# Gated linear attention with routed experts: a chunk's output products on quarters of TensorE's array, copied out by ScalarE, and the work behind them re-ordered

## The reference, cut to what matters

```
q = relu(x @ Wq)   16 heads of 64        k = relu(x @ Wk), v = x @ Wv   4 key heads of 64
g = log_sigmoid(x @ Wg1 @ Wg2 + b) / 16
S_t = exp(g_t) * S_(t-1) + k_t (outer) v_t ;  o_t = q_t @ S_t / 8
o = g_norm_weight * o * rsqrt(mean(o^2 over the head) + eps)
x = x + layernorm(o @ Wo)
x = x + layernorm(sum of the top-2 of 8 experts' gated MLPs of layernorm(x))
```

## Time and profile before

| | |
|---|---|
| median of 3 runs | 1224.97 us (1224.72 to 1226.8) |
| the profiled execution, its own time | 1229.17 us |
| its span in the trace | 1227.4 us |
| granted TensorE clock over the span | 0.984 of full speed |
| TensorE busy | 1159.2 us, 94% of the span |
| VectorE, ScalarE, GpSimd busy | 771.0, 651.1, 554.5 us |

### The profile page before, as it was taken

How to read it: one execution, slowest core, us unless ns; L and a number is a source line. 1 busy time by engine, 2 the same in 40 slices (tenths; PEclk the granted TensorE clock), 3 DMA queues, 4 the chain that set the end, 5 groups by cost and what they waited for, 6 DMA issues and landing times.

```text
span 1227.4 us, 29645 instructions
## 1 busy us (share of the span) xinstructions
PE 1159.2 (94%) x9166; PEld 988.5 (81%) x9166; DVE 771.0 (63%) x2380; ACT 651.1 (53%) x1653; POOL 554.5 (45%) x686
## 2 busy tenths in 40 slices
PE   8999999999999999999999999399999999999995
PEld 5888878878878788888788788389999999988862
DVE  5777877887887787778778878423333333333337
ACT  4656656557547557557566573234444444443336
POOL 2344564554654654644645644423333333333326
PEclk9999999999999999999999999689999999999998
DMA  7010110100101100101101101334111111111534
GB/s 281 10 28 12 32 44 9 34 26 25 34 17 30 39 17 26 43 13 30 43 11 32 34 9 64 116 107 116 50 49 48 50 45 52 47 48 43 180 116 190
DMA packets 59677, 67.51 MB, mean 55 GB/s; under 512 B 6896, under 2 KB 49664, under 8 KB 59264
## 3 DMA queue, kind: packets, MB, share of 16 engines
q1 hardware_dynamic: 48720, 41.10, 10.7%
q0 software_dynamic: 8448, 17.45, 4.3%
q10 hardware_dynamic: 2480, 8.61, 2.2%
HBM read 37.98 MB, written 29.15 MB: 55 GB/s over the span
## 4 chain that ended last, share of the span: by engine, by line
PE 73%; DVE 13%; ACT 5%; issue 5%; DMA 3%; POOL 1%; DVEq 0%; ACTq 0%; SPq 0%; POOLq 0%
PE pO L779 10%; PE pO L606 6%; PE pJ L561 6%; PE pW L639 5%; PE pO L611 5%; PE pA L590 5%; PE pA L770 4%; PE pA L771 4%; PE pJ L770 4%; PE pJ L771 4%; PE pT L622 3%; PE pA L561 2%; PE pJ L532 2%; PE pA L539 2%; PE pJ L519 2%
## 5 line engine op out<-in xcount | busy, mean ns | idle before, releaser
L1658 POOL DMA_INDIRECT expert_out<-y,tail x136 | 130.1, 957 | 262.8 <-ACT y L1040 239.3
L890 ACT ACTIVATE sq<-pO 128x512 f32<-128x512 f32 x128 | 76.0, 593 | 170.3 <-PE pO L606 118.7
L606 PEld LDWEIGHTS pO<-vJ,aT 128*128 128x128 f32 x1024 | 127.9, 192 | 27.1 <-issue 24.0
L606 PE MATMUL pO<-vJ,aT 128*128 128x128 f32 x1024 | 139.1, 279 | 5.5 <-DVE aT L1176 5.5
L1569 POOL DMA_INDIRECT expert_rows<-x1n,rowi x120 | 120.3, 1002 | 48.0 <-issue 29.7
L779 PE MATMUL pO<-wdown_sb,vJ 128*128 128x128 f32 x1088 | 133.9, 277 | 0.0
L779 PEld LDWEIGHTS pO<-wdown_sb,vJ 128*128 128x128 f32 x1088 | 128.2, 194 | 0.0
L1183 DVE TENSOR_REDUCE ss<-sq 128x8 f32<-128x512 f32 x128 | 86.4, 675 | 62.1 <-ACT sq L890 61.2
L1437 DVE TENSOR_TENSOR vJ<-pA,kJ 128x256 f32<-128x256 f32 x136 | 57.6, 425 | 107.9 <-ACT kJ L1029 107.5
L611 PE MATMUL pO<-S_mid,qT 128*128 128x128 f32 x896 | 118.3, 275 | 0.0
L611 PEld LDWEIGHTS pO<-S_mid,qT 128*128 128x128 f32 x896 | 109.0, 192 | 0.0
(11 more groups left out here) (234 smaller groups left out, 2432.1 us busy)
## 6 DMA issues: line engine op xcount, KB each, us to landing
xt<-expert_rows SPq DMA_DIRECT2D x69, 130.0 KB
...
```

The costliest lines, as they stand in the source:

```text
L606: last = mm(o[:, g, h, :, :], aT[:, c % 2, h, g * P:(g + 1) * P], vJ[:, c, h, :], start=(h == 0 and g == 0), stop=(c == 0), skip_group_che ...
L1658: g.indirect_dma_start(out=ys_dram, in_=y[:, k, :], in_offset=None, out_offset=bass.IndirectOffsetOnAxis(ap=tail[:, k, 1:2].bitcast(U32), ...
```

## The change

The output of a chunk is made of products of 64x64x64 on quarters of the array, each for one head and 64 rows, so that the zeros are no longer multiplied. It is written in two functions, since a row half of the array writes one of the two PSUM banks in the first and the other bank in the second: `first_outputs` (8 products) and `more_outputs` (8 more, and 16 with the state), which waits on `first_psum` until the first 8 have ended. Both banks of `pR` (columns 0 to 255, `head_bank`) hold one chunk's output, so there is only one such buffer now. ScalarE copies it to SBUF (`heads`, in the half of `S_mid` that is free now) ahead of its squares, and VectorE scales from there. The next chunk's first products wait for that copy (`heads_ready`) where they waited for VectorE's scaling of chunk `c - 2` (`on_ready`).

`out_transposes` moves from one chunk later to two, between `first_outputs` and `more_outputs`. `norm_transposes` moves to chunk 1, `gate_logits` follow the outputs of chunks 2 and 3, `ranks` moves from chunk 5 to chunk 6. `merge_heads` of tile 2 moves out of chunk 7 behind the keys and values of the next sequence. On ScalarE the gates' parts are spread over chunks 2 to 7, and `router_rstd` and `norm_T` stand behind `head_scale`. GpSimd writes `S_mid` in half the size, without `own_step`. The values lose their zero quarters in the same way (`vJ[..., 0:D]`).

```diff
+        heads = S_mid[:].rearrange("p n a (u v) -> p u (n a) v", u=2)[:, 1, :, :]
...
+        head_bank = pR[:, :, 0:4 * D]
...
-            def outputs(i, c):
+            def intra(c, p, h, g, r, start):
+                rows = slice(p * C, p * C + C)
+                head = 2 * g + r
+                return mm(head_bank[r * C:(r + 1) * C, h, (p * 2 + g) * D:(p * 2 + g + 1) * D],
+                          aT[rows, c % 2, h, head * C:(head + 1) * C], vJ[rows, c, h, 0:D],
+                          start=start, stop=(c == 0), skip_group_check=True)
+
+            def inter(c, p, h, g, r):
+                rows = slice(h * D, h * D + D)
+                return mm(head_bank[r * C:(r + 1) * C, h, (p * 2 + g) * D:(p * 2 + g + 1) * D],
+                          qT[rows, p, c, 2 * g + r, :], S_mid[rows, c, p, 0:D],
+                          start=False, stop=True, skip_group_check=True)
+
+            def first_outputs(i, c):
                 pe.wait_ge(a_ready, i * NC + c + 1)
-                if c >= 2:
-                    pe.wait_ge(on_ready, i * NC + c - 1)
+                if c > 0:
+                    pe.wait_ge(heads_ready, i * NC + c)
                 else:
                     pe.wait_ge(raw_ready, i * (NC - 1) + NC - 1)
+                settle(pe)
+                for g in range(2):
+                    for r in range(2):
+                        for p in range(2):
+                            last = intra(c, p, 1 - p, g, r, g == 0)
+                last.then_inc(first_psum, 1)
+
+            def more_outputs(i, c):
+                pe.wait_ge(first_psum, i * NC + c + 1)
                 if c > 0:
                     pe.wait_ge(mid_ready, i * (NC - 1) + c)
-                o = pO[c % 2][:].rearrange("t (p g) (h v) -> t g h p v", p=PAIRS, h=2)
-                for h in range(2):
-                    for g in range(2):
-                        last = mm(o[:, g, h, :, :], aT[:, c % 2, h, g * P:(g + 1) * P], vJ[:, c, h, :],
-                                  start=(h == 0 and g == 0), stop=(c == 0), skip_group_check=True)
-                for p in range(PAIRS):
-                    for g in range(2):
-                        if c > 0:
-                            last = mm(pO[c % 2][:, 2 * p + g, :],
-                                      qT[:, p, c, 2 * g:2 * g + 2, :].rearrange("p r c -> p (r c)"),
-                                      S_mid[:, c, p, :], start=False, stop=True, skip_group_check=True)
+                settle(pe)
+                for g in range(2):
+                    for r in range(2):
+                        for p in range(2):
+                            last = intra(c, p, p, g, r, False)
+                if c > 0:
+                    for p in range(PAIRS):
+                        for g in range(2):
+                            for r in range(2):
+                                for h in range(2):
+                                    last = inter(c, p, h, g, r)
                 last.then_inc(o_psum, 1)
...
                 scores(i, 0)
                 project_queries(i, 1, range(1, 2))
                 for c in range(NC):
-                    outputs(i, c)
-                    if c == 1:
-                        project_queries(i, 1, range(3, 4))
+                    first_outputs(i, c)
+                    if c >= 2:
+                        out_transposes(i, c - 2)
+                    more_outputs(i, c)
                     if more and c == 2:
-                        norm_transposes(i + 1, routed)
+                        gate_logits(i + 1, 0)
                     if c % 2 == 0 and c + 2 < NC:
                         scores(i, c + 2)
-                    if c == 0:
-                        project_queries(i, 1, range(2, 3))
-                    if c in (3, 5, 7):
-                        merge_heads(i, (c - 3) // 2, more)
-                    if c > 0:
-                        out_transposes(i, c - 1)
+                    if c < 2:
+                        project_queries(i, 1, range(2 + c, 3 + c))
+                    if more and c == 1:
+                        norm_transposes(i + 1, routed)
+                    if more and c == 3:
+                        gate_logits(i + 1, 1)
                     if routed and c == (3 if more else 2):
                         router_transposes(i - 1, i - 1, x1n)
-                    if more and c in (2, 3):
-                        gate_logits(i + 1, c - 2)
+                    if c in (3, 5):
+                        merge_heads(i, (c - 3) // 2, more)
                     if routed and c == (4 if more else 3):
                         logits(i - 1)
-                    if routed and c == (5 if more else 4):
+                    if routed and c == (6 if more else 4):
                         ranks(i - 1)
...
             def turn(i, routed):
                 chunks(i, True, routed)
-                project_keys(i + 1, routed)
+                out_transposes(i, NC - 2)
+                project_keys(i + 1, routed, range(0, 1))
+                project_values(i + 1)
+                project_keys(i + 1, routed, range(1, 2))
+                merge_heads(i, NT - 2, True)
+                key_transposes(i + 1)
                 out_transposes(i, NC - 1)
-                project_values(i + 1)
-                key_transposes(i + 1)
+                project_queries(i + 1, 0, range(0, 1))
+                state_updates(i + 1)
                 merge_heads(i, NT - 1, True)
-                state_updates(i + 1)
-                project_queries(i + 1, 0)
+                project_queries(i + 1, 0, range(1, 4))
...
             def squares(i, c):
                 act.wait_ge(o_psum, i * NC + c + 1)
-                a(sq[:, c % 2, :], pO[c % 2][:].rearrange("p k v -> p (k v)"), ACT.Square)\
+                if c >= 2:
+                    act.wait_ge(on_ready, i * NC + c - 1)
+                a(heads[:, c % 2 * 8:c % 2 * 8 + 8, :].rearrange("p (h k) d -> p h k d", h=2),
+                  head_bank.rearrange("p h (k d) -> p h k d", d=D), ACT.Copy).then_inc(heads_ready, 1)
+                act.wait_ge(heads_ready, i * NC + c + 1)
+                a(sq[:, c % 2, :].rearrange("p (n d) -> p n d", d=D), heads[:, c % 2 * 8:c % 2 * 8 + 8, :], ACT.Square)\
                     .then_inc(sq_ready, 1)
...
             def chunks(i, more, routed):
                 for c in range(NC):
+                    if c >= 2:
+                        out_T(i, c - 2)
                     squares(i, c)
                     if more and c == 0:
                         norm_rstd(i + 1)
                     if more and c == 2:
-                        norm_T(i + 1)
+                        gate_abs(i + 1, 0)
+                    if more and c == 3:
+                        gate_log(i + 1, 0)
+                    if more and c == 4:
+                        gate_exp(i + 1, 1)
+                    if more and c == 5:
+                        query_decays(i + 1, 0)
+                    if c in (4, 6):
+                        merged_rstd(i, (c - 4) // 2)
+                    if c == 7 and more:
+                        out_T(i, c - 1)
+                    if c == 7 and not more:
+                        router_rstd(i, i, HALVES[0])
+                    head_scale(i, c)
+
                     if routed and c == (2 if more else 1):
                         router_rstd(i - 1, i - 1)
-                    if c in (4, 6):
-                        merged_rstd(i, (c - 4) // 2)
-                    if more and c == 4:
-                        gate_exp(i + 1, 1)
-                    if more and c == 7:
-                        decays(i + 1, 1)
-                    if not more and c == 7:
-                        router_rstd(i, i, HALVES[0])
-                    if c == 6:
-                        out_T(i, c - 1)
-                    head_scale(i, c)
-                    if c > 0 and c != 6:
-                        out_T(i, c - 1)
-
+                    if more and c == 1:
+                        norm_T(i + 1)
                     if more and c == 2:
-                        gates(i + 1, 0)
-                        gate_logs(i + 1, 0)
+                        gate_relu(i + 1, 0)
+                        gate_exp(i + 1, 0)
...
                     mask(i, c + 2)
                 if last and c == NC - 1:
                     last_norm(i, HALVES[0])
+                if not last and c == NC - 1:
+
+                    dve.wait_ge(mid_ready, i * (NC - 1) + NC - 1)
+                    gate_steps(i + 1)
+                    keys(i + 1)
                 dve.wait_ge(rs_ready, i * NC + c + 1)
                 v.tensor_tensor(
-                    on[:, c % 2, :, :].rearrange("p k (h d) -> p (k h) d", d=D),
-                    pO[c % 2][:].rearrange("p k (h d) -> p (k h) d", d=D),
-                    wide(rs[:, c % 2, :].unsqueeze(2), P, 8, D), ALU.mult).then_inc(on_ready, 1)
...
             def queries_and_states(j, merging):
                 if merging is not None:
+                    query(j, 0, 0)
```

(19 more changed lines are left out.)

54 lines of the change are left out of this document (34 added, 20 removed).

## The result

The changed kernel takes 1316.82 us (median of 4 runs, 1314.27 to 1319.09); the kernel before takes 1225.88 us beside it (4 runs). The ratio is 1.074, 95% interval 1.0714 to 1.0766. The forecast was 1273 us in a range of 1240 to 1302: the direction was right, the size was not. The profiled execution took 1319.09 us with a span of 1317.3 us, 89.9 us more than the span before; the forecast had +48.

The account below looks back on a forecast made before the run. TensorE bounds the kernel, but after the change three chains set the turn: 34.4 + 16.4 = 50.8 us for 47.5, +46 us over 14 looped turns, 1277 us profiled, 1273 us against the median; range 1240 to 1302.

Parts of the forecast that it names:

- The walk from outputs to keys: Looped turn, from chunk 0's outputs to the next keys: 34.4 us, for 31.9 before.
- norm: TensorE ahead of the norm transposes: arrives at 5.4, rows `xn` only at 7.4, so it waits 2.0 us.
- router: TensorE ahead of the router transposes: arrives at 14.3, rows `x1n` only at 16.1, so 1.8 us of waiting.
- ahead of the keys: TensorE between `choose` and the next keys: idles about 3 us, no longer having the merge of tile 2.
- the quarter products' gain: Outputs on TensorE: 240 products at 37 ns, 8.9 us for 13.4; about 3 us a turn left after hand-overs.
- The 0.15 us given to each change between whole array and quarters: TensorE in the outputs: some 0.15 us for each of seven more changes, taken off the quarter products' gain.
- taken off are about 1.0 us: Keys to next outputs: 15.6 us plus the merge's 1.8, less about 1.0 of waits covered by the new order, 16.4.
- The last sequence: Last chunks, with no next sequence: 0 to +1 us.
- The experts: The experts' stage behind the turns: as before, no change in time.
- turn 0: First turn: has the first wait without the router's, +1.5 us.
- The rival of slow quarters: Outputs take 14.2 us if instruction stops come in every chunk or quarters don't run side by side: 1310 us, chance 0.12.
- The rival in which TensorE's saving comes through: The three waits together fall below 3 us, so a looped turn loses 3 us: 1180 us, chance 0.12.

Follow-up runs that it names:

- k13_keys: Changed kernel with norm transposes in chunk 2, tile 2's merge in chunk 7, squares before copy, tile 0's merge before router transposes, keys together before values: 1239.46 us, ratio 1.0074.
- k1_again: Changed kernel plus unused blank products each turn, 10 ahead of chunk 6's head transposes and 9 ahead of the next keys: 1306.99 us, ratio 1.062.
- k4_nointer: Changed kernel without the 16 products of qT by S_mid in each of chunks 1 to 7: ratio 1.0971.
- k14_best: As `k13_keys`, but ScalarE copies before squaring in chunk 6, and the last sequence's merge of tile 2 is back in chunk 7: ratio 1.0081.
- a_again: The changed kernel, unaltered, run once more in another batch: 1318.37 us, ratio 1.0719 to the kernel before.

## Why the prediction was right, and where it failed

The walk from outputs to keys was right: 34.6 us for 34.4, with the waits where it put them, 1.5 us for 2.0 (norm), 1.7 for 1.8 (router), 2.2 for 3 (ahead of the keys). The last is less since 0.75 us of idling stand earlier, ahead of the merge of tile 1, where the forecast had none. That the total came within 0.2 us is partly such trading of small waits. The size of the quarter products' gain was right too: 2.5 us of busy time for "about 3". A product took the 37 ns that it was given: the 16 records of a half in 0.28 us (8 products, 35 ns each), the 32 of `inter` in 0.58 us (36 ns). The 0.15 us given to each change between whole array and quarters stood on no row; what the trace shows is 0.59 us for the head transposes between two groups of quarters, for 0.44 between whole products before, so 0.15 for two changes.

The sum was 42 us short, in four terms; the first two are the steps that failed.

**The tail, 14 x 1.1 = 15 us.** The step that said "taken off are about 1.0 us" failed. K to C is 17.5 us for a forecast of 16.4, against 15.6 before: the merge's 1.8 us in full and nothing back. The waits that the new order should cover are there: 0.39 ahead of the outputs, 0.34 before, and 0.80 for `qT`. Turn 0 has neither of them, and its tail too is 1.8 us longer than before. What the merge did cover, the wait for `kT`, exists only since the order parts the two key products; `k13_keys` shows it. Together with 0.2 in C to K the turn is 52.1 for 50.8, 17 us in the 14 turns of the window, as the first of them begins with turn 0's shorter tail.

**The clock, 15 us in the turns and 3 behind them.** The forecast had no term for it. It let TensorE idle three times a turn and priced each at its own length. Nine drops of 1.6 to 1.7 us follow, and the last sequence has two. `k1_again` took six of nine away and got 10.2 us back; in `k4_nointer` they became longer and more frequent as work was removed.

**The last sequence, 4 us.** It takes 8.2 us more from keys to the experts' first tile (82.3 for 74.1), about 3 of them drops; the forecast had 0 to 1. Part of it is the merge, which stands later there too: `k14_best` puts it back, and that stretch takes 73.6 us for 76.8 in `k13_keys`.

**The experts, 3.6 us.** They were held to be as before, and stand at 431.1 us for 427.6. `a_again` has 428.8, `k14_best` 431.8, `k13_keys` 434.0, `k1_again` 440.9. The traces show where it varies. TensorE is busy 409.5 us of it in `k13_keys` for 404.9 before, at a granted clock of 0.97 for 0.98, with the same 2378 records; and its waits for the experts' rows are 29.6 us in `k1_again` for 20.6 in `a_again`. Why the clock and these transfers differ was not settled.

Against these stands turn 0, forecast +1.5 and measured -0.3. The sum: 17 + 15 + 3 + 4 + 4 - 2 = 41, and the rest is rounding.

The rival of slow quarters gave 1310 us, near the result, for a reason that is not there. The rival in which TensorE's saving comes through asked for the three waits together below 3 us; they were 5.4. (The lower end of the range counts five microseconds of waits where the walk has 6.8.) What fails a range like this one is a cost that was in no case, neither the likeliest nor a rival.
